# Projection and finish pieces of an attention layer as 64x32 tiles: row halves in two banks, added by the vector engine

## What is computed

```python
x = x + attention(layernorm(x))     # qkv projection, softmax, out projection
x = x + ffn(layernorm(x))           # tanh(h @ W @ A1 @ A2 + bias)
```

## Time and profile before

| What | us |
|---|---|
| three executions | 2202.97, 2204.01, 2208.4 (median 2204.01) |
| the profiled execution's own time | 2206.76 |
| its span, from the first to the last instruction | 2202.9 |
| what lies around the span | 3.9 |

### The profile page before, as it was taken

The page is one execution under the profiler, slowest core; times in us unless marked ns, Lnnn a source line. Parts: engine busy times, 40 slices in busy tenths (PEclk is TensorE's granted clock), DMA queues, the critical chain, the costliest instruction groups (busy, mean ns, idle before and its releaser), DMA issues. The chain is left out here.

```text
span 2202.9 us, 76197 instructions
## 1 busy us (share of the span) xinstructions
PE 1903.6 (86%) x34896; PEld 677.2 (31%) x34896; DVE 587.1 (27%) x1206; ACT 1987.1 (90%) x2106; POOL 149.9 (7%) x172
## 2 busy tenths in 40 slices
PE   6698998989889898999889899898988888888882
PEld 4232332323323233333323333232332222222221
DVE  5221323223222332323223232222311111111212
ACT  3499999999889999999889999999989999999990
POOL 2000101001000000101001010100100000000000
PEclk9799999999999999999999999999999999999995
DMA  3410102011240111102331010201123010101000
GB/s 120 128 31 15 44 24 63 25 54 31 44 81 24 54 33 34 44 12 63 53 67 48 24 43 24 64 24 44 32 41 64 15 44 14 44 15 34 16 23 27
DMA packets 84927, 92.81 MB, mean 42 GB/s; under 512 B 15786, under 2 KB 73578, under 8 KB 84594
## 3 DMA queue, kind: packets, MB, share of 16 engines
q1 hardware_dynamic: 84596, 87.83, 16.0%
HBM read 53.09 MB, written 26.25 MB: 36 GB/s over the span
## 5 line engine op out<-in xcount | busy, mean ns | idle before, releaser
L1113 ACT ACTIVATE probs<-scores 128x1024 f32<-128x1024 f32 x2048 | 1948.6, 1056 | 117.8 <-PE scores L1135 80.7
L1154 PE MATMUL outs<-probs,vs 64*32 64x512 f32 x16384 | 1081.0, 593 | 7.7 <-issue 7.7
L1135 PE MATMUL scores<-qs,ks 49*32 49x512 f16 x16384 | 839.9, 384 | 231.2 <-ACT probs L1113 180.7
L1135 PEld LDWEIGHTS scores<-qs,ks 49*32 49x32 f16 x16384 | 233.4, 89 | 1250.6 <-ACT probs L1113 1093.5
L1154 PEld LDWEIGHTS outs<-probs,vs 64*32 64x32 f32 x16384 | 291.2, 106 | 74.3 <-issue 30.7
L837 DVE TENSOR_TENSOR probs<-probs,allowed 128x320 f32<-128x320 f32 (+2 forms) x280 | 138.6, 495 | 388.1 <-ACT probs L1113 388.1
L1195 PE MATMUL spare<-s_xt,w_qkv 128*128 128x512 f32 x192 | 108.0, 645 | 0.0
L786 POOL TENSOR_TENSOR s_squares<-s_qk_f 128x512 bf16<-128x512 f32 x48 | 61.4, 1279 | 464.1 <-DVE s_qk_f L897 464.1
L1237 PE MATMUL spare<-w_o,ctx_in 128*128 128x256 f32 x256 | 74.1, 416 | 19.0 <-DVE ctx_in L862 19.0
L897 DVE TENSOR_SCALAR s_qk_f<-spare,bias_qk 128x512 f32<-128x512 f32 x48 | 36.0, 751 | 182.1 <-PE spare L1195 182.1
L1257 PE MATMUL spare<-w_ffn,s_f_xt 128*128 128x256 f32 x256 | 74.0, 415 | 0.8 <-DVE s_f_xt L977 0.8
(11 more groups left out here) (97 smaller groups left out, 566.5 us busy)
## 6 DMA issues: line engine op xcount, KB each, us to landing
qs<-q_parts SPq DMA_DIRECT2D x192, 64.0 KB
ks<-k_parts SPq DMA_DIRECT2D x36, 256.0 KB
ctx_in<-raw SPq DMA_DIRECT2D x256, 32.0 KB, 2.0
s_x<-in_x SPq DMA_DIRECT2D x16, 512.0 KB, 4.0
inverse<-row_inverse SPq DMA_DIRECT2D x32, 256.0 KB
out<-s_pre SPq DMA_DIRECT2D x16, 512.0 KB, 2.9
s_xin<-in_x SPq DMA_DIRECT2D x12, 512.0 KB, 6.0
q_parts<-s_parts SPq DMA_DIRECT2D x24, 256.0 KB, 2.1
```

The source lines that it names most:

```text
L1113: act.activation(probs[:, u % RING, 2 * slot:2 * slot + 2].rearrange("p c q -> p (c q)"), scores[:, 2 * slot:2 * slot + 2].rearrange("p c ...
L1135: last = pe.matmul(scores[cols, 2 * slot + e], ks[rows, group, keys], qs[rows, group], start=True, stop=True)
L1154: last = pe.matmul(outs[32 * c:32 * c + 32, side], vs[keys, at:at + 2 * HD], probs[keys, u % RING, c], start=(i == 0), stop=(i == KBLOCKS ...
```

## The change

Every piece becomes a set of matmuls on 64x32 tiles, the shape that weighing has. The 128 rows of a contraction are split in two halves: the upper half sums in `spare[0]`, the lower in `spare[1]`, and a second DVE instruction adds the two (`take_qk`, `take_v`, `take_norms`, `add_attention`, `add_f_bias`). A transpose becomes a matmul with the identity (`turned_tiles`); the two banks then hold the two row halves of each tile of 128 tokens, and `copy_turned` puts them side by side.

The pieces are smaller and more: queries and keys 16 (before 8), values 8 (4), turning 4 and 4 (2 and 2), output 8 (4), FFN 8 (4), norms 1 (1). Their unit numbers are constants now. They come in groups of four with a unit without a piece behind each; units 13 and 45 have none. `head_of` gets 32 columns, of which 16 are used. In steps that project, the finish's last part moves past the step's end: its transposes to units 56 to 59, its FFN pieces to 61 to 64 and 66 to 69, squash to 72, the final sum to 74, so into units 0 to 10 of the next step. SP therefore stores a result one step later and loads x for the finish after `invert_sums`; `move_context` of the first head group comes ahead of the key parts' `store_part`. The FFN folding moves from units 22 and 50 of step 0 to 23 and 28. DVE's inverse moves from unit 7 to 8, scaling of the context from 13, 14 to 19, 20.

The core of the diff (left out are the new semaphores, `head_of`, the DVE's and PE's `run_step`, which follow the constants, and the two `f_` functions that repeat the form of others):

```diff
+TURN_AT = (7, 8, 9, 10)
+QK_AT = ((12, 14, 15, 16), (18, 19, 20, 21), (33, 34, 35, 36), (38, 39, 40, 41))
+FOLD_AT = (23, 28)
+Y_AT = ((23, 24, 25, 26), (28, 29, 30, 31))
+V_AT = ((43, 44, 46, 47), (51, 52, 53, 54))
+NORM_AT = 49
+F_TURN_AT = {True: (56, 57, 58, 59), False: (41, 42, 43, 44)}
+F_AT = {True: ((61, 62, 63, 64), (66, 67, 68, 69)), False: ((47, 48, 49, 50), (52, 53, 54, 55))}
+SQUASH_AT = {True: 72, False: 58}
...
+        def finishing(step, r):
+
+
+            found = []
+            for c, at in ((step - 1, r), (step - 2, r + STEP)):
+                if c >= 0:
+                    found.append((c, at, c + 1 < PROJECTED))
+            return found
+
         block = ctx.enter_context(nc.Block())
...
                     invert_sums(step - 1)
+                    if step > 1:
+                        store_result(step - 2)
+                    start_chunk(step - 1)
                 if projects:
                     if step + 1 < PROJECTED:
-                        sp.wait_ge(turned, step * 2 + 2)
+                        sp.wait_ge(turned, step + 1)
                         sp.dma_start(xin[:], x_tiles[CPB + step + 1]).then_inc(x_in, 16)
                     store_part(step, 0)
                     store_part(step, 1)
                 if step + 1 < NCH and not qc == CPB - 1:
                     sp.wait_ge(scored, 2 * STEP * step + STEP)
                     load_queries(sp, lay, step + 1, 0, q_parts)
+                move_context(step, 0)
                 if projects:
                     store_part(step, 2)
                     store_part(step, 3)
-                move_context(step, 0)
                 if projects and qc == CPB - 1:
                     sp.wait_ge(scored, 2 * STEP * step + STEP)
                     sp.wait_ge(parts_out, (step + 1) * 64)
...
                     sp.wait_ge(guard_done, b + 1)
                     load_guards(sp, lay, 0, guard)
-                if step:
-                    store_result(step - 1)
-
             sp.dma_start(xin[:], x_tiles[CPB]).then_inc(x_in, 16)
             for dst, src in ((a1t, a1_t), (a2s, a2), (w1t, w1_t)):
                 sp.dma_start(dst, src.rearrange("(h p) n -> p h n", p=P)).then_inc(ffn_in, 16)
             for step in range(NCH):
                 run_step(step)
...
+            def copy_turned(step):
+                dve.wait_ge(turned, step + 1)
                 if step:
                     dve.wait_ge(v_ready, step * 2)
-                dve.tensor_copy(xt[:, half], spare[half][:]).then_inc(turn_copied, 1)
+                for part in range(2):
+                    dve.tensor_copy(xt[:].rearrange("p k (t r i) -> p r k t i", r=2, i=HALF_P)[:, part],
+                                    spare[part][:].rearrange("p (k t i) -> p k t i", k=HALVES, t=TPC)
+                                    ).then_inc(turn_copied, 1)
 
...
+                dve.tensor_scalar(qk_f[:, j % 2], spare[0][:], scale, bias_qk[:, j:j + 1], ALU.mult, ALU.add
+                                  ).then_inc(qk_added, 1)
+                dve.wait_ge(qk_added, n + 1)
+                dve.scalar_tensor_tensor(out=qk_f[:, j % 2], in0=spare[1][:], scalar=scale, in1=qk_f[:, j % 2],
+                                         op0=ALU.mult, op1=ALU.add).then_inc(qk_copied, 1)
                 dve.wait_ge(qk_copied, n + 1)
                 if step:
...
+                    "p (k n d) -> p k n d", k=4, d=V_COLS)[:, :, :, 0:HD]
                 dve.tensor_tensor(
-                    lay["vs"][b % 2][:, at:at + 4 * V_ROW].rearrange(
-                        "p (k n d) -> p k n d", k=4, d=V_COLS)[:, :, :, 0:HD],
-                    spare[1 - half][:].rearrange("p (k n d) -> p k n d", k=4, d=HD),
+                    columns, spare[0][:].rearrange("p (k n d) -> p k n d", k=4, d=HD),
                     keep["bias_v"][:].rearrange("p (n d) -> p n d", d=HD).unsqueeze(1).to_broadcast(
-                        [P, 4, HALVES * HG, HD]), ALU.add).then_inc(v_copied, 1)
+                        [P, 4, HALVES * HG, HD]), ALU.add).then_inc(v_added, 1)
+                dve.wait_ge(v_added, step * 2 + half + 1)
+                dve.tensor_tensor(columns, columns, spare[1][:].rearrange("p (k n d) -> p k n d", k=4, d=HD),
+                                  ALU.add).then_inc(v_copied, 1)
...
+                both = qk_f[0:HALF_P, 0]
                 dve.wait_ge(norms_ready, step + 1)
                 if b and qc == 0:
                     dve.wait_ge(max_done, 2 * b)
+                dve.tensor_copy(both, spare[0][0:HALF_P]).then_inc(norms_added, 1)
+                dve.wait_ge(norms_added, 2 * step + 1)
+                dve.tensor_tensor(both, both, spare[1][0:HALF_P], ALU.add).then_inc(norms_added, 1)
+                dve.wait_ge(norms_added, 2 * step + 2)
                 for w in range(2):
-                    dve.tensor_reduce(qk_sq[:, w, qc:qc + 1], spare[0][32 * w:32 * w + HEADS], AX.X,
+                    dve.tensor_reduce(qk_sq[:, w, qc:qc + 1], qk_f[32 * w:32 * w + HEADS, 0], AX.X,
                                       ALU.max).then_inc(norms_copied, 1)
 
...
             def add_attention(c, pair):
                 dve.wait_ge(biased, c + 1)
-                dve.wait_ge(y_ready, c * TPC + 2 * pair + 2)
-                dve.tensor_tensor(x2[:, 2 * pair:2 * pair + 2], x2[:, 2 * pair:2 * pair + 2],
-                                  spare[pair][:].rearrange("p (t e) -> p t e", t=2), ALU.add).then_inc(x2_done, 1)
+                dve.wait_ge(y_ready, c * 2 + pair + 1)
+                tiles = x2[:, 2 * pair:2 * pair + 2]
+                dve.tensor_tensor(tiles, tiles, spare[0][:].rearrange("p (t e) -> p t e", t=2), ALU.add
+                                  ).then_inc(y_added, 1)
+                dve.wait_ge(y_added, c * 2 + pair + 1)
+                dve.tensor_tensor(tiles, tiles, spare[1][:].rearrange("p (t e) -> p t e", t=2), ALU.add
+                                  ).then_inc(x2_done, 1)
...
+            def turned_tiles(tiles, pair, k):
+
+
+                for t in (2 * pair, 2 * pair + 1):
+                    for c in range(4):
+                        for part in range(2):
+                            rows = slice(part * HALF_P, part * HALF_P + HALF_P)
+                            at = (k * TPC + t) * HALF_P
+                            last = pe.matmul(spare[part][32 * c:32 * c + 32, at:at + HALF_P],
+                                             tiles[rows, t, k * P + 32 * c:k * P + 32 * c + 32], ident[rows, rows],
+                                             start=True, stop=True)
+                return last
+
+            def product(at, weights, moving, k):
+
+
+                for c in range(4):
+                    for part in range(2):
+                        rows = slice(part * HALF_P, part * HALF_P + HALF_P)
+                        last = pe.matmul(spare[part][32 * c:32 * c + 32, at:at + EMB], weights(rows, c), moving[rows],
+                                         start=(k == 0), stop=(k == HALVES - 1))
+                return last
+
+            def turn(step, i):
+                if i == 0:
+                    pe.wait_ge(xn_done, step * 2 + 2)
+                    if step == 1:
+                        pe.wait_ge(v_copied, 2)
                     if step > 1:
                         pe.wait_ge(pre_done, step * 2 - 2)
-                for t in range(TPC):
-                    last = pe.transpose(spare[half][:, t * P:(t + 1) * P], xin[:, t, half * P:(half + 1) * P], ident[:])
-                last.then_inc(turned, 1)
-
-            def project_qk(step, j, k):
-                if k == 0:
-                    if j < 2:
+                last = turned_tiles(xin, i // 2, i % 2)
+                if i == 3:
+                    last.then_inc(turned, 1)
+
...
+                last = product(n * EMB, lambda rows, c: w_qkv[rows, k, j * P + 32 * c:j * P + 32 * c + 32],
+                               xt[:, k, n * EMB:(n + 1) * EMB], k)
+                if i == 3:
                     last.then_inc(qk_ready, 1)
 
-            def project_v(step, two):
-                if two == 0:
-                    pe.wait_ge(qk_copied, step * 4 + 4)
-                if two == 2:
-                    if step:
-                        pe.wait_ge(f_turn_copied, step * 2 - 1)
+            def project_v(step, half, i):
+                if i == 0:
+                    if half == 0:
+                        pe.wait_ge(qk_copied, step * 4 + 4)
                     else:
-                        pe.wait_ge(norms_copied, 2)
-                for kb in (2 * two, 2 * two + 1):
-                    for k in range(HALVES):
-                        for side in range(2):
-                            last = pe.matmul(spare[1 - two // 2][side * HALF_P:(side + 1) * HALF_P,
-                                                                 kb % 4 * P:(kb % 4 + 1) * P],
-                                             xt[:, k, kb * KEYS:(kb + 1) * KEYS],
```

(89 more changed lines are left out.)

254 lines of the change are left out of this document (104 added, 150 removed).

## The result

The changed kernel takes 2111.4 us (median of four, 2106.0 to 2112.9) against 2203.5 us: ratio 0.958, 95% interval 0.955 to 0.960. The forecast was 2120 us, in a range from 2086 to 2172. The profiled execution took 2111.1 us, with a span of 2106.8.

A forecast was written before the change was run, and what follows sets the result against it. ACT's exponentials were taken to bound the kernel, with PE's pieces delaying them. Steps -114, instruction fetch +24 and tail +7 us sum to -83: 2123.8 us profiled, 2121 as median, rounded to 2120, range 2086 to 2172 us.

The forecast's parts named there:

- What bounds the kernel: ACT's exponentials, 0.916 us from start to start; a plain unit of 1.83 us leaves PE a gap of 0.51 us.
- Price of the pieces: On PE, query, key, output and FFN pieces take 0.43 us, value and turning pieces 0.5 us, inside the gap.
- The rival with 0.028 us a pair: Value and turning pieces take 0.88 us on PE, over the gap: +50 us in all, 2170 us; chance 0.12.
- A step's length: A projecting step takes 119.2 us instead of 127.7; all steps together save 114 us.
- The handover rival: PE waits for DVE's delayed adds at group ends: 10 us a step, 2235 us, slower; chance 0.08.
- Instruction fetch: At the six key loads PE runs out of instructions sooner; each stall grows some 4 us, +24 us in all.
- SP's order: Loading x for the finish later and storing key parts behind the context costs nothing.
- The tail: After the last unit, waits for DVE's two adds and dearer turning add 7 us (3 to 12).
- The sum: Whole kernel: -114 + 24 + 7 = -83 us, 2123.8 us profiled, less 2.8 to the median, rounded to 2120.

The follow-up runs named there:

- e1_wide: Changed kernel with its schedule and both banks, but pieces on wide tiles again (128x128, value pieces 128x64); 2216.0 us, 1.0045 of the kernel before.
- e4_one_sum: Changed kernel without DVE's second adds, so sums lack the lower half of each contraction; 2104.2 us, ratio 0.954.
- e6_no_empty: Changed kernel with the empty unit removed after some query, key, output and FFN groups, four places a step; 2117.8 us, ratio 0.961.
- e3_spread: Changed kernel with the DMAs of the six key loads issued one every two units instead of all at once; 2072.9 us, ratio 0.940.
- e5_before_spread: Kernel before the change, with the DMAs of the six key loads spaced as in e3_spread; 2171.8 us, ratio 0.985.
- e2_joined: Changed kernel with narrow tiles, but two pieces in one unit and none in the next; 2145.5 us, ratio 0.972.
- e8_spread_again: e3_spread run once more, unchanged, for comparison with a version that has a wide tail; 2070.4 us, ratio 0.941.

## Why the prediction was right, point by point

**What bounds the kernel.** Right. ACT's pace of 0.916 us and a gap of about 0.5 us for PE carried the whole estimate: with pieces inside the gap, units with and without pieces take the same 1.83 us (step 10 against step 13: both 118.68 us, with 49 pieces and with 20).

**Price of the pieces.** Right for queries, keys, output and FFN (0.433 us, 0.43 expected) and for values (0.436 us by columns, 0.5 taken). The turning piece is 0.318 us, not the 0.22 of its columns nor the 0.5 taken: its 32 pairs start over 0.31 us, 0.010 us a pair. Both prices fit the gap, so the misses cost nothing. The rival with 0.028 us a pair falls by this. So does the rule of the Trainium skill, TensorEngine Tiling (Array Packing), "Instruction Overhead", as the prediction applied it: 60 cycles for each of 32 matmuls in turn would be 0.80 us, an estimate from that page. The turning pieces take 0.32; for tiles side by side the trace disagrees with it. That the extra 0.3 us belong to the shape was argued before and is shown by e1_wide: the same columns and unit numbers, 0.33 + 0.63 us with wide tiles against 0.22 + 0.43 us. How they divide between first weights and emptying the array, no run shows.

**A step's length.** 119.2 us forecast, 118.68 measured; 0.5 us had been set aside for late handovers, and there are none in such a step: it is no longer than step 13, which has 20 pieces for 49, and no shorter without the second adds (e4_one_sum). -114 us forecast for all steps, -118.2 measured.

**The handover rival.** It fell: with the empty unit PE never comes late. Without it (e6_no_empty) a wait of 0.44 us costs ACT 0.35 us, so a delay would have cost less than the rival charged.

**Instruction fetch.** Right in kind and direction: +24 us forecast, +16.7 measured; of six stops of 9 to 11 us that were to be seen, four came (9.5, 9.5, 9.6 and 11.3 us), the other two were 7.3 and 5.0 us. The mis-sized term is the time that PE lives on what it has: taken as 290 instructions at 47 a us, 6 us from the load; it was 476 at 52 a us, 9.1 us. Behind it is a miscount: a unit has 16 pairs for scores and 16 for weighing, 32 and not 24 (a step of the kernel before has 2188 matmuls in all, of which 140 are pieces), so 64 instructions and not 48. Both the store and the rate came out too low, and the quotient hid most of it: that this term was no further off is in part luck. What PE has in hand also differs with when its last packet came, from 0.1 us behind the load (476) to 2.6 us ahead of it (403 before the change).

The cause is shown from three sides: no packet of instructions moves in the last 7 us or more before PE stops, and one starts just before it goes on; spacing the loads takes most of the stops away in both kernels (e3_spread, e5_before_spread); and fewer instructions at the same places make the sum of the stops smaller (e1_wide, 31 against 52 us). By the Trainium skill, Runtime: NRT & Kernel Launch, "Instruction fetch mechanics", the fetch would be mostly hidden. Outside the six loads the trace agrees: `stream` has no other wait for "issue" of over 1.5 us before a matmul. At the loads it disagrees, by 2.7 to 7.1 us each.

**SP's order.** Loads of x take 6.9 us to land instead of 4.0, and cost nothing, as forecast: POOL waited for them for 655 us, and no engine waited for POOL's sum.

**The tail.** +7 us forecast, +4.9 measured. The wait (1.66 and 1.57 us) and the second add (0.69 us) were right, but output and FFN got only 1.7 and 1.9 us longer, not 2.5 each: the narrow groups took less than the wide ones, 3.57 + 1.96 us against 6.25 for output. The forecast left that out, and it hangs on the granted clock of the moment. Turning cost 0.7 us where 1 to 2 were taken.

**The sum.** The three terms were off by 4.2, 7.3 and 2.1 us, all in the same direction: the profiled execution was forecast at 2123.8 us and took 2111.1, 12.7 us less. The forecast then took off 2.8 us for the step to the median, which here lies 0.3 us over the profiled execution; so 2120 stands 8.6 us over 2111.4 where the working itself was 12.7 us off.

## What to carry to other kernels

Where small tiled matmuls fill most of the time on PE, a wide matmul between them pays beyond its columns, here 0.3 us; cast it in the shape of its neighbours and cut it to fit the gap that the bounding engine leaves. Do both: the shape alone brought two thirds (e2_joined), and the spreading with wide tiles nothing as built (e1_wide), in part because its turning pieces had become dearer. And where a stall has "issue" before PE in the middle of a group, look at what the DMA queues carry: spacing a bulk load that is not urgent was worth another 39 us, and the version with that and a wide tail ran in 2063 us, 0.939 of the kernel before.

## What the runs showed of the hardware

- A change between 32-wide tiles and 128-wide ones costs 0.3 us with a float32 piece of 256 columns, 0.1 us before its first matmul and 0.2 us behind its columns (e1_wide against the changed kernel).
- 32 pairs of a weight load and a matmul on eight tiles go through in 0.32 us, 0.010 us from start to start (the turning piece).
- Turning with 128-wide weights and 64 moving columns costs 1.03 us for eight passes that start 0.12 us apart (e1_wide); with 128 moving columns the passes of the kernel before start 0.13 us apart. So the columns don't set it, and the weight loads are what is left, though no run tells them apart. With 32-wide weights it is 0.32 us.
- A 16 KB packet of instructions (6.09 MB in 372) that finds the DMA engines full comes too late: PE stops for 2.4 to 5.7 us before the change and 2.7 to 7.1 us after it, where it uses more instructions a microsecond.
- In the tail PE starts again after 19 us of idleness at a granted clock of 0.53 (0.50 in e8_spread_again), the level of 1.2 GHz. A group of 64 narrow matmul instructions takes 3.6 us then and 1.96 us at a granted clock of 1.00, 2.4 GHz. In the changed kernel the second output group was at the higher level, in e8_spread_again it was still at the lower, 3.67 us, so the same code's tail differs by 1.7 us from this alone.
